# An attention, scan and expert pipeline on one core: query, key and value projections placed elsewhere, and the stages up to the first scan put in another order

## The chip, the cores and the metric

The kernel runs on one core of a Trainium2 chip. The metric is the device time of one execution, in microseconds (us); lower is better. Before the change three runs took 1169.0, 1170.27 and 1170.85 us, median 1170.27 us.

## What is computed

Two layers over four batches of 512 tokens with 256 features, all in float32. The part that matters here is the head of layer 0:

```
qkv = x @ w_qkv.T + b_qkv                    # 4 batches, 16 heads of 16
attn = softmax(q @ k.T / 4)                  # 512 x 512 for each head
h = (attn @ v) @ w_out.T + b_out
h = concatenate([h, txt])                    # 512 + 77 tokens
u = layernorm(h); xp = u @ x_proj_w.T
delta = softplus(xp[..., :64] @ dt_proj_w.T + dt_proj_b)
state = exp(delta * A) * state + delta * B * u       # scan over 589 tokens, 16 states
h = h + sum(state * C) + u * D_skip
```

Behind it come an expert layer of 14 experts (layer 0), a causal attention and an expert layer of 128 experts with two experts per token (layer 1). The change doesn't touch them.

## The kernel before

Every engine has its own program, written out by hand; semaphores join them. Nothing is reordered by a scheduler: on each engine an instruction that waits holds up everything behind it.

For each batch `b` the heads are worked in four groups `hg` of four heads, and a group in four units of 128 queries (16 units a batch, `NU`). A unit has two **sets** `g` of two heads; a set fills two of PSUM's eight banks. The steps are:

- **Projections** (TensorE, `project`, L657): Q (`which` 0) and K (`which` 1) of a group, two matmuls each (four passes in the trace); ScalarE evicts them with their bias (`take_q`, L1251). V comes in two halves (`project_v`, L667; `take_v`, L1255). x of a batch lies in the one tile `xT`, and SP loads the next batch's over it once all projections of the batch are made (`load_x`).
- **Scores and maxima**: `scores` (L686) makes a set, VectorE takes its negated row maxima (`maxima`, L1682). With three bank sets (`SETS`) TensorE may be three sets ahead; for most of batch 1 there are only two sets. After a group, `turn_maxima` (L701) transposes the maxima and `minus` (L1687, VectorE) adds them to Q's spare rows.
- **Turned scores and weighted sums**: `tscores` (L766) makes the scores again, transposed and with the maximum taken off, `exps` (L1305, ScalarE) takes the exponential, `weighted` (L779) multiplies with V into bank 4, and `take_o` (L1309) evicts it after a group. `turn_heads` (L796), `values`, `turn_values`, `project_out` and `residual` (L1762, VectorE) finish the attention.
- **Chain to the scan**: `moments`, `standard_deviations`, `normalise`, `turn_tokens` (L711), `take_u`, `project_x` (L718), `take_x`, `project_dt` (L725), `softplus` (L1281 to L1288, ScalarE), `step_size` (L1710), `input_size`.
- **Scan** (VectorE): for each of 16 states `drive` (L1724), `recurrence` (L1733) and `output_gate` (L1743); `decay` (L1296, ScalarE) makes its factors, SP broadcasts its rows.

The stages, with their functions: `first_front` (scores and maxima of batch 0 with its projections), `first_back` (turned scores of batch 0, with batch 1's projections and first scores), `first_chain` (the rest of batch 0's chain between the scores of batch 1, units 4 to 15), `back_ahead(1, 0)` (the scan of batch 0 on VectorE, while TensorE and ScalarE do the turned scores of batch 1), then `front(2, 1)`, `back_ahead(2, 1)`, `front(3, 2)`, `back_ahead(3, 2)`, the last scan, and the later layers. In `front(mb, nb)` VectorE takes all the maxima of batch `mb`, while TensorE also turns y of batch `nb - 1` at units 7, 9 and 11 (`turn_both`, L843). `back_ahead` projects Q and K of the next batch's groups 0 to 2 near its end, into banks 5 to 7; group 3 and V are projected in the front.

In the first front both projections of the next group stand whole behind units 1 and 2:

```
if i in (1, 2):
    if hg + 1 < HG:
        project(b, hg + 1, i - 1)
    else:
        project_v(b, i - 1)
```

## Time and profile before

| | |
|---|---|
| median of three runs | 1170.27 us |
| the profiled execution | 1173.3 us, span 1171.5 us |
| TensorE matmul busy | 918.4 us, 78% of the span |
| TensorE weight load busy | 505.3 us, 43% |
| VectorE busy | 762.7 us, 65% |
| ScalarE busy | 443.0 us, 38% |
| GpSimd busy | 204.6 us, 17% |
| mean granted TensorE clock | 0.849 of full |

The shares are averages over stages with different limits. The span is the time from the first to the last instruction of the profiled execution; its own time, 1173.3 us, is 1.8 us more. In the rows below, PE is TensorE's matmul, PEld its weight load, DVE VectorE, ACT ScalarE, SP the engine that issues most DMAs. A float32 matmul has two passes and so two entries.

### The profile page before, as it was taken

What the parts mean: (1) busy time and instruction counts of PE and PEld (TensorE: products, weight loads), DVE (VectorE), ACT (ScalarE), POOL (GpSimd) and SP (SyncE); (2) the same over time, 40 slices, a digit from 0 to 9 for tenths busy, and PEclk for the clock granted to TensorE, in tenths of its full rate; (3) what the DMA queues carried; (4) which work ended last, traced back from release to release, by engine and by line L of the source; (5) the groups of instructions that cost most, each with busy time, mean ns of one, the idle gap of its engine ahead of it and who ended that gap; (6) DMA issues with size and microseconds to landing.
All of it is one profiled execution on the core that took longest, in us unless ns stands there. A gap on an engine that the chain in (4) does not pass through costs nothing. (4 is left out here: it accounts for less than half of the span.)

```text
span 1171.5 us, 14347 instructions
## 1 busy us (share of the span) xinstructions
PE 918.4 (78%) x4632; PEld 505.3 (43%) x4633; DVE 762.7 (65%) x1351; ACT 443.0 (38%) x822; POOL 204.6 (17%) x248
## 2 busy tenths in 40 slices
PE   7899889978988888975576539999489898529980
PEld 2323432242522434223353239999266666414440
DVE  4802569999799997999899931111366767833325
ACT  1156226952169521783452214444123313302220
POOL 1000000111001100011000142333000023246660
PEclk9989877986879869796686859999699988759995
DMA  3099123987039760487666446665600500229957
GB/s 104 11 334 319 59 83 101 216 197 169 1 110 236 182 155 1 119 217 182 178 205 210 146 154 190 196 199 161 242 1 1 218 22 15 75 81 376 400 206 264
DMA packets 75403, 185.57 MB, mean 158 GB/s; under 512 B 12154, under 2 KB 48717, under 8 KB 72656
## 3 DMA queue, kind: packets, MB, share of 16 engines
q1 hardware_dynamic: 60944, 148.11, 37.9%
q0 software_dynamic: 14400, 36.71, 14.4%
q8 instruction: 33, 0.54, 0.2%
q14 instruction: 26, 0.21, 0.1%
HBM read 124.88 MB, written 43.69 MB: 144 GB/s over the span
## 5 line engine op out<-in xcount | busy, mean ns | idle before, releaser
L1682 DVE TENSOR_REDUCE mxn<-ps 128x2 f32<-128x1024 f32 x128 | 150.3, 1219 | 92.2 <-PE ps L686 92.0
L1733 DVE TENSOR_TENSOR_SCAN hst<-dA,dBu 128x1180 f32<-128x1180 f32 x64 | 166.9, 2608 | 0.5
L1305 ACT ACTIVATE Ph<-ps 128x1024 f32<-128x1024 f32 x128 | 125.5, 1075 | 37.1 <-PE ps L766 36.6
L686 PE MATMUL ps<-Kh,Qh 32*128 32x512 f32 x512 | 118.8, 750 | 16.7 <-DVE mxn L1682 13.2
L766 PE MATMUL ps<-Qh,Kh 32*128 32x512 f32 x512 | 118.6, 732 | 1.9 <-ACT Ph L1305 1.8
L1724 DVE TENSOR_TENSOR dBu<-dtu,bc 128x1180 f32<-128x1180 f32 x64 | 88.1, 1381 | 6.7 <-DMA bc<-bc_dram 6.3
L1619 POOL DMA_DIRECT2D yS<-hC x24 | 20.8, 866 | 409.4 <-DVE hC L1743 409.4
L1743 DVE TENSOR_TENSOR hC<-hst,bc 128x1180 f32<-128x1180 f32 x64 | 86.8, 1362 | 0.0
L2043 DVE TENSOR_TENSOR yo<-ps,b2r 128x256 f32<-128x256 f32 x32 | 13.6, 424 | 105.9 <-PE ps L1020 105.9
L1296 ACT ACTIVATE dA<-delta,acol 128x590 f32<-128x590 f32 x64 | 52.2, 816 | 71.3 <-DVE hst L1733 63.2
L779 PE MATMUL ps<-Ph,Vh 128*32 128x512 f32 x512 | 74.1, 653 | 5.2 <-ACT OT L1309 3.3
L1221 PE MATMUL ps<-ring,xgT 128*64 128x256 f32 x512 | 71.0, 400 | 0.1
L2300 DVE COPY yo<-ps 128x256 f32<-128x256 f32 x64 | 27.2, 424 | 66.6 <-PE ps L1221 66.6
L657 PE MATMUL ps<-xT,wqk 128*128 128x512 f32 x128 | 63.7, 637 | 7.4 <-DMA wqk<-in_wqk 5.2
L1671 POOL DMA_INDIRECT ys_dram<-yo,dest x64 | 62.3, 973 | 40.2 <-issue 23.5
L1651 POOL DMA_INDIRECT xs_dram<-xa,to x40 | 39.6, 989 | 167.4 <-DVE to L2142 154.8
L766 PEld LDWEIGHTS ps<-Qh,Kh 32*128 32x128 f32 x512 | 35.5, 207 | 77.0 <-ACT Ph L1305 41.7
L686 PEld LDWEIGHTS ps<-Kh,Qh 32*128 32x128 f32 x512 | 35.3, 214 | 76.2 <-DVE mxn L1682 49.3
L1010 PEld LDWEIGHTS ps<-xgT,W 128*128 128x128 f32 x512 | 63.4, 195 | 3.2 <-ACT xgT L1450 1.6
L1010 PE MATMUL ps<-xgT,W 128*128 128x128 f32 x512 | 63.9, 279 | 1.0 <-ACT xgT L1450 1.0
L788 PE MATMUL ps<-hC,ident 128*128 128x512 f32 (+1 forms) x96 | 47.7, 647 | 18.2 <-DVE hC L1743 18.2
L1020 PE MATMUL ps<-W,hidT 128*128 x256 | 60.5, 380 | 0.0
(266 smaller groups left out, 1428.8 us busy)
## 6 DMA issues: line engine op xcount, KB each, us to landing
bc<-bc_dram SPq DMA_DIRECT2D x64, 590.0 KB, 5.1
ring<-in_we SPq DMA_DIRECT2D x16, 2048.0 KB, 14.0
W<-in_w SPq DMA_DIRECT2D x46, 512.0 KB, 4.0
yS<-hC POOLq DMA_DIRECT2D x24, 590.0 KB, 6.9
yodd<-hC POOLq DMA_DIRECT2D x24, 590.0 KB, 7.1
xs_dram<-zeros SPq DMA_DIRECT2D x1, 8224.0 KB, 42.7
xg<-xs_dram SPq DMA_DIRECT2D x16, 514.0 KB, 10.9
ys_dram<-zeros SPq DMA_DIRECT2D x1, 5120.0 KB, 47.6
```

The lines of the kernel that those rows point to most:

```text
L657: m = nc.tensor.matmul(ps[:, bank, :], wqk[:, hg, which, c, :], xT[:, c, :], start=(c == 0), stop=(c == KC - 1))
L686: m = nc.tensor.matmul(ps[:, banks.start + hh % 2, :], Qh[HR * hh:HR * (hh + 1), hg, P * i:P * (i + 1)], Kh[HR * hh:HR * (hh + 1), hg, :], ...
L766: m = nc.tensor.matmul(ps[:, banks.start + hh % 2, :], Kh[HR * hh:HR * (hh + 1), hg, P * j:P * (j + 1)], Qh[HR * hh:HR * (hh + 1), hg, :], ...
L779: m = nc.tensor.matmul(ps[HR * hh:HR * (hh + 1), 4, :], Vh[:, j, 4 * hg + hh, :], Ph[:, n % 2, hh, :], start=(j == 0), stop=(j == QT - 1))
L1010: m = nc.tensor.matmul(ps[:, 2 + u, P * f:P * (f + 1)], W1[:, v, c, P * f:P * (f + 1)], xgT[:, u, c, :], start=(c == 0), stop=(c == KC - 1))
L1221: t = nc.tensor.matmul(ps[CAP * k:CAP * (k + 1), 2 + j % 4, 0:D], xgT5[:, j % 2, c, CAP * k:CAP * (k + 1)], weights_of(g % PLACES)[:, 2 * ...
L1305: nc.scalar.activation(Ph[:, n % 2, 2 * g:2 * g + 2, :], ps[:, turned_banks(b, 2 * n + g), :], ACT.Exp, scale=float(HD) ** -0.5).then_inc( ...
L1671: nc.gpsimd.indirect_dma_start(ys5_dram, bass.IndirectOffsetOnAxis(dest5[:, j:j + 1], 0), yo5[:, j // GP % YG, j % GP, :], None, bounds_ch ...
L1682: nc.vector.tensor_reduce(slots32(mxn[:, hg % 2, i, :])[:, 2 * g:2 * g + 2, HD], ps[:, score_banks(b, 2 * u + g), :], AX.X, ALU.max, negat ...
L1724: nc.vector.tensor_tensor(dBu[:, k % 2, :, :], dtu[:, :, :], bc[:, k % SLOTS, 0:1, :].to_broadcast([P, KC, LP]), ALU.mult).then_inc(dve_dB ...
L1733: nc.vector.tensor_tensor_scan(hst[:, k % 2, :, :].rearrange("p c t -> p (c t)"), dA[:, k % 2, :, :].rearrange("p c t -> p (c t)"), dBu[:, ...
L1743: nc.vector.tensor_tensor(gated(k), hst[:, k % 2, :, :], bc[:, k % SLOTS, 1:2, :].to_broadcast([P, KC, LP]), ALU.mult).then_inc(dve_hC, 1)
```

## The change

Seven things, all in the order of the programs and in the PSUM banks:

1. `project` and `project_v` are cut into parts of one matmul (`project_part`) and one tile pair (`project_v_part`); in the first front one part stands behind each unit. Batch 0's maxima are turned in bank 7, its projections stay in bank 4.
2. Batch 0's turned scores wait for the last maxima of their own banks, not for all; units 0 to 7 use three bank sets. The turn of group 3's maxima stands behind unit 0's turned scores.
3. `turn_heads` of group 3 comes behind a set of batch 1's scores.
4. In the first chain Q3 and K3 of batch 1 stand inside units 5 and 6, `project_dt` is cut in two around a set of scores, V's halves stand behind units 9 and 10 (before: 13 and 14), and VectorE's `step_size` and `input_size` behind units 12 and 13 (before: 10 and 11).
5. For batches 2 and 3, Q3 is projected behind Q and K of groups 0 to 2, K3 behind `turn_tokens`, and V's first half behind `project_dt`, all in `back_ahead` of the batch ahead.
6. V's second half stands behind unit 0 in `front`.
7. ScalarE's evictions follow: `take_v(mb, 0)` behind `softplus`, `take_v(mb, 1)` first in the front.

The core of the diff:

```
+        def q_bank(b, hg, which):
+            if b == 0:
+                return 4 if hg else which
+            if b == 1:
+                return 7
+            return gap_bank(hg, which) if hg < QG else (4, 3)[which]
+
+        def v_bank(b):
             return 7 if b == 1 else 4
+
+        def turn_bank(b):
+            return 7 if b < 2 else 4
...
+        def turned_set(b, v):
+            return SETS[v % 2] if b == 0 and v >= NU else SETS[v % 3]
...
+            def project_part(b, hg, which, c):
+                bank = q_bank(b, hg, which)
+                if c == 0:
+                    if hg == 0 and which == 0:
...
+                    elif b >= 2:
+                        if which == 0:
+                            pe.wait_ge(act_ot, HG * b)
+                        else:
+                            pe.wait_ge(dve_vals, 2 * b)
...
+            def project_v_part(b, half, i):
+                if i == 0:
+                    if half:
+                        pe.wait_ge(act_v, 2 * b + 1)
+                    elif b == 0:
+                        pe.wait_ge(act_q, 2 * HG)
+                    elif b >= 2:
+                        pe.wait_ge(act_q, 2 * (HG * b + QG) + 1)
...
+                elif b >= 2 and v == 1:
+                    pe.wait_ge(act_q, 2 * HG * (b + 1))
...
+                if b < 2 and hg:
+                    pe.wait_ge(dve_q, HG * b + hg)
+                if b == 1:
+                    if hg > 1:
+                        pe.wait_ge(act_v, 2 * b + 2)
+                    else:
+                        pe.wait_ge(act_q, 2 * (HG * b + QG + hg))
+                elif b >= 2:
                     pe.wait_ge(act_v, 2 * b + 2)
...
+                    if hg + 1 < HG:
+                        project_part(b, hg + 1, i // 2, i % 2)
+                    else:
+                        project_v_part(b, i // 2, i % 2)
...
-                if n == 0:
+                if n == 0 and b:
...
-                    if v >= turned_sets(b):
-                        pe.wait_ge(act_p, 2 * NU * b + v + 1 - turned_sets(b))
+                    if turned_free(b, v):
+                        pe.wait_ge(act_p, turned_free(b, v))
+                    elif b == 0:
+                        pe.wait_ge(dve_max, last_maxima(b, v))
...
+                    else:
+                        turn_maxima(0, HG - 1)
...
-                turn_heads(0, range(HG))
+                turn_heads(0, range(QG))
+                scores(1, 4, 0)
+                turn_heads(0, range(QG, HG))
 
             def first_chain():
-                scores(1, 4, 0)
-                turn_maxima(1, 0)
                 turn_values(0, 0)
                 turn_values(0, 1)
                 scores(1, 4, 1)
+                turn_maxima(1, 0)
                 project_out(0, 0)
                 project_out(0, 1)
-                unit_scores(1, 5)
-                unit_scores(1, 6)
+                scores(1, 5, 0)
+                project(1, 3, 0)
+                scores(1, 5, 1)
+                scores(1, 6, 0)
+                project(1, 3, 1)
+                scores(1, 6, 1)
                 turn_tokens(0, low)
                 unit_scores(1, 7)
                 project_x(0, low)
+                scores(1, 8, 0)
                 turn_maxima(1, 1)
-                unit_scores(1, 8)
-                unit_scores(1, 9)
-                project_dt(0, low)
-                project(1, 3, 0)
+                scores(1, 8, 1)
+                project_dt_part(0, low, 0)
+                scores(1, 9, 0)
+                project_dt_part(0, low, 1)
+                scores(1, 9, 1)
+                project_v(1, 0)
                 unit_scores(1, 10)
-                project(1, 3, 1)
-                unit_scores(1, 11)
-                for u in range(12, NU):
+                project_v(1, 1)
+                for u in range(11, NU):
                     unit_scores(1, u)
                     if u == 12:
                         turn_maxima(1, 2)
-                    elif u in (13, 14):
-                        project_v(1, u - 13)
                 turn_maxima(1, 3)
...
-                    if i in (1, 2):
-                        if hg + 1 == QG:
-                            project(mb, QG, i - 1)
-                        elif hg + 1 == HG:
-                            project_v(mb, i - 1)
+                    if u == 0:
+                        project_v(mb, 1)
...
+                    project(eb + 1, QG, 0)
                 room = low if eb == NB - 1 else tail
                 turn_tokens(eb, room)
+                if eb < NB - 1:
+                    project(eb + 1, QG, 1)
                 project_x(eb, room)
                 project_dt(eb, room)
+                if eb < NB - 1:
+                    project_v(eb + 1, 0)
...
             def first_chain():
                 take_vals(0, 0)
                 take_vals(0, 1)
+                take_q(1, 3, 0)
                 standard_deviations(0)
                 normalise(0)
+                take_q(1, 3, 1)
                 take_u(0, low)
                 take_x(0, low)
                 softplus(0, low)
-                take_q(1, 3, 0)
-                take_q(1, 3, 1)
-                begin_sum(0)
                 take_v(1, 0)
                 take_v(1, 1)
+                begin_sum(0)
                 decay(0, 0)
 
             def front(mb, nb):
+                take_v(mb, 1)
                 decay(nb, 0)
-                take_q(mb, 3, 0)
-                take_q(mb, 3, 1)
-                take_v(mb, 0)
                 begin_sum(nb)
-                take_v(mb, 1)
 
...
+                            take_q(eb + 1, QG, 0)
                     if n == 13:
                         take_u(eb, room)
+                        if eb < NB - 1:
+                            take_q(eb + 1, QG, 1)
                     if n == 14:
                         take_x(eb, room)
                 softplus(eb, room)
-                if eb == NB - 1:
+                if eb < NB - 1:
+                    take_v(eb + 1, 0)
+                else:
...
-                maxima(1, 4, 0)
+                unit_maxima(1, 4)
                 minus(1, 0)
-                maxima(1, 4, 1)
                 residual(0)
                 moments(0)
                 maxima(1, 5, 0)
...
                     unit_maxima(1, u)
                     if u % QT == 0:
                         minus(1, u // QT - 1)
-                    if u == 10:
+                    if u == 12:
                         step_size(0)
-                    elif u == 11:
+                    elif u == 13:
                         input_size(0)
```

How the rows of TensorE's program move, at three places. In the first front (from the turn of group 0's maxima to that of group 1's, with group 2's projections; L657 and L682 are Q and K projections, L686 and L729 scores, L701 and L749 the turn of maxima), before:

```order
L701 MATMUL ps<-ident,mxn 128x128 x4
L686 MATMUL ps<-Kh,Qh 128x512 x4
L657 MATMUL ps<-xT,wqk 128x512 x2
L686 MATMUL ps<-Kh,Qh 128x512 x4
L657 MATMUL ps<-xT,wqk 128x512 x2
L686 MATMUL ps<-Kh,Qh 128x512 x8
L701 MATMUL ps<-ident,mxn 128x128 x4
```

and now:

```order
L749 MATMUL ps<-ident,mxn 128x128 x4
L682 MATMUL ps<-xT,wqk 128x512
L729 MATMUL ps<-Kh,Qh 128x512 x4
L682 MATMUL ps<-xT,wqk 128x512
L729 MATMUL ps<-Kh,Qh 128x512 x4
L682 MATMUL ps<-xT,wqk 128x512
L729 MATMUL ps<-Kh,Qh 128x512 x4
L682 MATMUL ps<-xT,wqk 128x512
L729 MATMUL ps<-Kh,Qh 128x512 x4
L749 MATMUL ps<-ident,mxn 128x128 x4
```

Each of the two projections has become two parts, one behind each of the group's four units.

In the first chain (L711 and L759 turn the tokens, L718 and L766 project x, L725 and L772 project dt), before:

```order
L711 MATMUL ps<-ident,xn 128x128 x10
L686 MATMUL ps<-Kh,Qh 128x512 x4
L718 MATMUL ps<-uT,xpw 96x512 x2
L718 MATMUL ps<-uT,xpw 96x78 x2
L701 MATMUL ps<-ident,mxn 128x128 x4
L686 MATMUL ps<-Kh,Qh 128x512 x8
L725 MATMUL ps<-xpo,dtw 128x512
L725 MATMUL ps<-xpo,dtw 128x78
L725 MATMUL ps<-xpo,dtw 128x434
L725 MATMUL ps<-xpo,dtw 128x156
L657 MATMUL ps<-xT,wqk 128x512 x2
L686 MATMUL ps<-Kh,Qh 128x512 x4
```

and now:

```order
L682 MATMUL ps<-xT,wqk 128x512 x2
L729 MATMUL ps<-Kh,Qh 128x512 x4
L682 MATMUL ps<-xT,wqk 128x512 x2
L729 MATMUL ps<-Kh,Qh 128x512 x2
L759 MATMUL ps<-ident,xn 128x128 x10
L729 MATMUL ps<-Kh,Qh 128x512 x4
L766 MATMUL ps<-uT,xpw 96x512 x2
L766 MATMUL ps<-uT,xpw 96x78 x2
L729 MATMUL ps<-Kh,Qh 128x512 x2
L749 MATMUL ps<-ident,mxn 128x128 x4
L729 MATMUL ps<-Kh,Qh 128x512 x2
L772 MATMUL ps<-xpo,dtw 128x512
```

The projections of Q3 and K3 have moved from behind dt to before the turn of the tokens, and a set of scores stands wherever two blocks stood together; the second half of dt and V follow.

At the end of the first scan and the start of front 2 (L667 and L701 with wv are V), before:

```order
L657 MATMUL ps<-xT,wqk 128x512 x12
L711 MATMUL ps<-ident,xn 128x128 x10
L718 MATMUL ps<-uT,xpw 96x512 x2
L718 MATMUL ps<-uT,xpw 96x78 x2
L725 MATMUL ps<-xpo,dtw 128x512
L725 MATMUL ps<-xpo,dtw 128x78
L725 MATMUL ps<-xpo,dtw 128x434
L725 MATMUL ps<-xpo,dtw 128x156
L686 MATMUL ps<-Kh,Qh 128x512 x20
L701 MATMUL ps<-ident,mxn 128x128 x4
L686 MATMUL ps<-Kh,Qh 128x512 x12
```

and now:

```order
L682 MATMUL ps<-xT,wqk 128x512 x14
L759 MATMUL ps<-ident,xn 128x128 x10
L682 MATMUL ps<-xT,wqk 128x512 x2
L766 MATMUL ps<-uT,xpw 96x512 x2
L766 MATMUL ps<-uT,xpw 96x78 x2
L772 MATMUL ps<-xpo,dtw 128x512
L772 MATMUL ps<-xpo,dtw 128x78
L772 MATMUL ps<-xpo,dtw 128x434
L772 MATMUL ps<-xpo,dtw 128x156
L701 MATMUL ps<-wv,xT 128x256 x4
L729 MATMUL ps<-Kh,Qh 128x512 x4
L701 MATMUL ps<-wv,xT 128x256 x4
```

Two matmuls more (Q3) stand in the run of projections, K3 behind the turned tokens, V's halves around unit 0's scores.

## Rows read from the trace of the kernel before

**Rows 1.** Busy time by stage: stretch, its length, each engine's busy time, clock, DMA.
```profile
core 0: us, PE busy (x) PEld busy (x) DVE busy (x) ACT busy (x) POOL busy (x), PEclk, DMA share, GB/s
13.60:59.70 46.10, 39.98 (x182) 15.35 (x181) 39.25 (x36) 5.32 (x8) 0.00 (x0) 1.00 0.05 14
...
89.00:121.40 32.40, 32.40 (x184) 10.23 (x180) 9.46 (x8) 19.44 (x23) 0.00 (x0) 1.00 1.08 324
...
121.40:183.30 61.90, 52.40 (x210) 24.91 (x210) 38.93 (x52) 18.04 (x28) 0.00 (x0) 0.80 0.15 52
...
183.30:273.30 90.00, 76.78 (x358) 27.97 (x350) 87.28 (x69) 65.47 (x87) 12.59 (x15) 0.86 0.74 176
...
268.40:286.00 17.60, 13.58 (x42) 4.16 (x41) 17.60 (x14) 6.52 (x8) 2.58 (x3) 0.59 0.88 204
```

**Rows 2.** Waits of VectorE, 14-60, 123-183, 273-329 us: total, times, longest.
```profile
DVE mxn L1682 <- PE ps L686: 6.5, 9, 0.9
...
DVE mxn L1682 <- PE ps L686: 18.6, 9, 7.9
...
DVE mxn L1682 <- PE ps L686: 8.1, 4, 3.9
```

**Rows 3.** Timeline, first front: start, duration, engine, line, what, [idle before <- releaser].
```profile
25.63 0.66 PE L701 MATMUL ps<-ident,mxn 128*128 128x128 f32 x4
...
30.39 1.14 PE L686 MATMUL ps<-Kh,Qh 32*128 32x512 f32 x8
...
31.47 1.98 PE L657 MATMUL ps<-xT,wqk 128*128 128x512 f32 x4
...
33.38 1.99 PE L686 MATMUL ps<-Kh,Qh 32*128 32x512 f32 x12
...
34.23 0.31 PEld L686 LDWEIGHTS ps<-Kh,Qh 32*128 32x128 f32 x4 [0.54 <-ACT Kh L1251]
...
34.55 4.62 DVE L1682 TENSOR_REDUCE mxn<-ps 128x2 f32<-128x1024 f32 x4 [0.63 <-PE ps L686]
...
39.09 0.68 DVE L1687 TENSOR_TENSOR Qh<-Qh,ps 128x512 f32<-128x512 f32 x1
```

**Rows 4.** Timeline, from the first front to the first back stage.
```profile
59.66 0.59 PE L701 MATMUL ps<-ident,mxn 128*128 128x128 f32 x3 [2.45 <-DVE mxn L1682]
...
62.58 1.94 ACT L1305 ACTIVATE Ph<-ps 128x1024 f32<-128x1024 f32 x2 [5.80 <-PE ps L766]
```

**Rows 5.** Timeline, units 3 to 8 of the first back stage.
```profile
75.93 1.07 PE L779 MATMUL ps<-Ph,Vh 128*32 128x512 f32 x8
...
76.93 1.98 PE L657 MATMUL ps<-xT,wqk 128*128 128x512 f32 x4
...
88.44 1.95 PE L766 MATMUL ps<-Qh,Kh 32*128 32x512 f32 x8 [0.27 <-ACT Ph L1305]
```

**Rows 6.** Timeline, first chain, up to the first scan.
```profile
123.30 1.13 PE L686 MATMUL ps<-Kh,Qh 32*128 32x512 f32 x4
...
150.97 4.46 PE L725 MATMUL ps<-xpo,dtw 64*128 64x512 f32 x8
...
155.37 3.78 PE L657 MATMUL ps<-xT,wqk 128*128 128x512 f32 x4
...
159.41 1.19 ACT L1288 ACTIVATE sp<-sp 128x1180 f32<-128x1180 f32 x1
...
160.25 2.36 DVE L1682 TENSOR_REDUCE mxn<-ps 128x2 f32<-128x1024 f32 x2 [7.93 <-PE ps L686]
...
162.52 1.38 DVE L1710 SCALAR_TENSOR_TENSOR delta<-xb,sp 128x1180 f32<-128x1180 f32 x1
...
183.29 2.68 DVE L1724 TENSOR_TENSOR dBu<-dtu,bc 128x1180 f32<-128x1180 f32 x2
```

**Rows 7.** Timeline, end of the first scan and front of batch 2.
```profile
272.46 1.19 ACT L1288 ACTIVATE sp<-sp 128x1180 f32<-128x1180 f32 x1
...
305.28 1.88 PE L657 MATMUL ps<-xT,wqk 128*128 128x512 f32 x4
...
308.26 2.35 DVE L1682 TENSOR_REDUCE mxn<-ps 128x2 f32<-128x1024 f32 x2 [2.66 <-PE ps L686]
```

More of the change, by code:

```diff
@@ new lines, in project @@
+            def project(b, hg, which):
+                for c in range(KC):
+                    project_part(b, hg, which, c)
+            def project_v_part(b, half, i):
[7 more added lines that the diff above has]
+                    else:
+                        pe.wait_ge(dve_q, HG * b + (HG - 2 if b == 1 else HG - 1))
+                for c in range(KC):
+                    m = nc.tensor.matmul(ps[:, v_bank(b), D * i:D * (i + 1)], xT[:, c, P * (2 * half + i):P * (2 * half + i + 1)], wv[:, c, :],
+                                         start=(c == 0), stop=(c == KC - 1))
+                if i == 1:
+                    m.then_inc(pe_v, 1)
@@ L669, in project_v @@
-                m.then_inc(pe_v, 1)
+                    project_v_part(b, half, i)
             def scores(b, u, g):
@@ L677, in scores @@
                     pe.wait_ge(dve_max, freed_by(b, v))
+                elif b == 1 and v == 0:
+                    pe.wait_ge(act_p, NU - 1)
                 elif b == 1 and v == 2 * QT + 1:
@@ L1245, in take_q @@
             def take_q(b, hg, which):
-                if b >= 2 and hg < QG:
-                    bank = gap_bank(hg, which)
-                else:
-                    bank = which if b == 0 and hg == 0 else misc_bank(b)
+                bank = q_bank(b, hg, which)
                 act.wait_ge(pe_q, 2 * (HG * b + hg) + which + 1)
```

91 lines of the change are left out of this document (42 added, 49 removed).

## Prediction

> **What bounds the kernel now.** I read the table of busy time by stage first. From 13.6 to 59.7 us VectorE, which takes the row maxima of batch 0's scores, works 39.3 of 46.1 us; in the first chain (121.4 to 183.3 us) 38.9 of 61.9; in the first scan (183.3 to 273.3 us) 87.3 of 90.0 [rows 1]. So a scan is bound by VectorE itself, while the stages ahead of the first scan have time in which it only waits. The page's chain of waits does not help: it names only the last stages. The later stages follow from the first scan without slack, so what the first 183 us lose or win should reach the end whole.
>
> The view of waits says for whom VectorE waits: for TensorE's scores, 6.5 us in the first front, 18.6 in the first chain, 8.1 in each later front [rows 2]. The reader should see in the timeline how: VectorE needs about 1.15 us for a set (4.62 for four), TensorE 1.08 for a unit of two sets and then 1.91 for a whole projection in between (from 31.47 to 33.38), and after it VectorE has stood still, for 0.63 us before the four maxima at 34.55 [rows 3]. In between, from 88.44 to 121.4 us, TensorE is busy all the time: 32.4 of 32.4 us [rows 1, 5].
>
> **First front.** Each projection of batch 0 is now made in two parts, one after each unit. Full and half clock (1.98 and 3.78 us for four passes) say that 1.80 of the time goes with the clock and some 0.15 is fixed [rows 3, 6], so a part costs 1.05, between 0.96 (half of 1.91) and 1.08. TensorE's period for a group of four units: 4 x 1.08 + 4 x 1.05 + 0.66 for turning the maxima + 0.85 of waiting until ScalarE has evicted K (the row at 34.23 against the next issue at 33.38) = 10.0 [rows 3]. VectorE's: 8 x 1.14 (from 34.55 to 39.09 for four) + 0.6 to 0.7 = 9.7 [rows 3]. So TensorE is still 0.3 too slow in the first three groups. Of the nine waits, 6.5 us in all [rows 2], the one before the very first maxima stays (a ninth, 0.7), and of the 5.8 left some 0.6 do, two of the three times 0.3: **-5.2**, bounds -4.0 and -5.8.
>
> **Switch and first half of the back stage.** Before, the last maximum ends at 59.6, its turn is made, the first exponential starts at 62.58 [rows 4], and the scores of unit 8 start at 88.44 [rows 5]: 28.8 us. Now the first turned scores wait for the last maxima only of their own banks, the turn comes after them, and three bank sets serve units 0 to 7 in place of two. From the last maximum: 1.15 for the second set, 0.66 for the turn, 7 x (1.07 + 1.00) for scores and weighted products (starts of 75.93 and 76.93 differ by 1.00), 2 x 1.91 for the projections of batch 1 [rows 3, 5] = 20.1. I add 1.9: 1.0 for unit 8, whose first set now waits for the exponential of unit 7's second set, and 0.9 for ScalarE's evictions. That is 22.0: **-6.8**, bounds -4 (the old pace returns after the start) and -8.7 (nothing added). Units 8 to 15 keep their two sets and TensorE their bound: 0.
>
> **First chain.** Its worst wait is 7.93 us at 160.25: TensorE has made the whole dt projection (4.46 at half clock) and a projection of Q (3.78) with no scores ready for VectorE [rows 6]. Now Q3 and K3 stand before the chain's token turn, dt comes in two halves, and V's halves stand at units 10 and 11. I walked the order from W, the end of the last weighted product, at full clock, with 1.91 for a projection, 1.08 for a pair of sets and as much for a set alone (the row at 123.30 has one set in 1.13, the one at 30.39 two in 1.14) [rows 3, 6], and half of the half-clock duration for other blocks. Heads are turned at W+3.0, about 1.1 later than before, since a set of scores is put between; outputs at 10.6; units 5 and 6, split around Q3 and K3, end at 19.1; tokens 20.6; x 24.0; dt 30.2. Then the first V half may be read only after ScalarE's softplus, about 5.2 us (from the end of dt at 155.43 to 160.60) [rows 6]: V's second half starts at 36.0, unit 11's scores end at 39.0. Behind them ten maxima (11.4), two subtractions, two operations of 1.4 on the step size and the last turn: the first drive of the scan at W+55.4 against 61.9 before (121.4 to 183.3) [rows 1, 6]. That is -6.5 at full clock. The old stage had a granted clock of 0.80 [rows 1]; the new one fills the gap behind the residual with Q3, so it should be better off, yet I leave 1.5: **-5.0**, bounds -1 (half clock in the long blocks again) and -8.
>
> **Ends of scans, fronts 2 and 3.** Q3, K3 and V0 go to the end of the preceding scan, behind the projections that are made there. They cost nothing there: TensorE waits for ScalarE around the token turn, and the scan is VectorE's; ScalarE's three evictions, under 0.85 us each, fit, since each decay is made a whole step of the scan (90.0 / 16 = 5.6 us) ahead [rows 1, 3]. SP's queue gains: the load of the next x no longer waits until the middle of the front. In the front the 1.88 us projection ahead of the wait of 2.66 us at 308.26 goes; what is late next there is the turn of y, so I keep 0.8 of it; of the two small waits (8.1 - 3.9 - 2.66 = 1.5) I take 0.6 [rows 2, 7]: -2.5. Against it stands a new wait: V's second half is the second thing in the front, and it needs V's first half evicted, which ScalarE does only behind the softplus that ends at 273.65 (272.46 + 1.19), so at 274.3 [rows 7]. Behind it on TensorE stand unit 1's scores, for which VectorE comes at 277.0 (two maxima and the step size after 273.3). At full clock V takes 1.9 and the scores 1.1: 277.4, a loss of 0.5. At half clock V takes 3.7 and the scores 1.1 to 1.7: 279.5, a loss of 2.6. I take half clock, since the clock granted from 268.4 to 286.0 is 0.59 although TensorE was busy 13.6 of these 17.6 us [rows 1]: +2.5. Per front **0**, bounds -2.5 and +1.5.
>
> The Trainium skill says otherwise: on its page "TensorE: Matmul & The Clock Gate", section "What's actually happening", the throttled clock is the default and activity releases it. By that V, which comes soon after an unbroken run of projections, would find 2.4 GHz, and both fronts together would give 4 us more; the trace of this place, 0.59 (the level of 1.2 GHz most of the time) right after such a run, speaks for the low level.
>
> **Sum.** -5.2 - 6.8 - 5.0 + 0 = -17.0. The profiled execution took 1173.3 us (span 1171.5), 3.0 above the median of the three runs; I carry the difference over to the median: 1170.3 - 17.0 = **1153.3**.
>
> **Rivals.**
> - *The chain gives little.* TensorE falls to half clock in the new chain too, at the wait for softplus or in the split units; each projection of 1.91 then costs 1.9 more. For it speaks the old stage's 0.80 [rows 1], against it the shorter waits. The chain gives 1 and the switch 5: 1170.3 - 11.2 = 1159.
> - *The fronts win.* V's second half meets the full clock: 1153.3 - 4 = 1149.3. This is also the time by the skill's rule.
> - *The shift does not arrive.* A transfer with a time of its own (the zero fill, the broadcasts) sets the scan's start: 1170. Against it: the DMA share in the old chain is 0.15, so the fill is long over [rows 1].
> - *Slower.* In the first front TensorE now goes between 32-row score matmuls and full ones twice as often. If that drops the granted clock there from 1.00 to 0.5, a group costs 4 x 1.7 + 4 x 1.95 + 1.3 + 0.85 = 16.8 in place of some 11.2 now (9.7 and a quarter of the waits), so +22 over four groups instead of -5.2: 1170.3 + 22 - 11.8 = 1180. With 5.6 lost in each slow group and 1.3 won in each other, it decides from the third slow group of the four. Against it: the old front, with as many kinds of matmul and less work, had 1.00 all along [rows 1].
>
> **How the numbers follow.** Forecast 0.56 (1149.5 to 1157), the chain gives little 0.20, the fronts win 0.16, no arrival 0.04, slower 0.04. The bounds of the terms added fully would reach from 1142 to 1165; as they will not all fall on one side, I cut to 1146 to 1162, which leaves out no change, slower, and a tenth beside. A change of 0.2%, 2.3 us, is about what a measurement of this kernel can tell from none. Faster 0.92, same 0.04, slower 0.04.
>
> **What would show it.** Right: the turn of batch 0's last maxima near 54.3 us, waits of VectorE below 1.5 us in that front; unit 8's turned scores near 76; the first drive of the scan near 166, with no wait of VectorE above 3 us in the chain; in fronts 2 and 3 the wait of 2.66 gone, and a wait of 0.5 to 3 us before unit 1's maxima. The scans keep their 90 and 88 us. Wrong: a granted clock under 0.9 in the first front, scores of units 0 to 7 still 3 us apart, or a scan that grows by what the stages before it won.

## The result, and the profile after

The changed kernel took 1155.52 us (median of four runs, 1148.68 to 1157.98) and the kernel before 1170.56 us on the same chip (four runs, 1169.0 to 1176.12): a ratio of 0.9869, 95% interval 0.9828 to 0.9911. That is 15.3 us faster, between 10.5 and 20.1. The forecast was 1153.3 us.

The profiled execution of the changed kernel is its fastest run, 1148.68 us (span 1146.8, mean granted clock 0.868), and that of before was above its median, so the two traces differ by 24.7 us. I use the traces for where the time went, and the ratios for how much. The table of busy time by stage, which answers to [rows 1]: first front, the two halves of the back stage, first chain, scan, front 2, scan, front 3.

```profile
core 0: us, PE busy (x) PEld busy (x) DVE busy (x) ACT busy (x) POOL busy (x), PEclk, DMA share, GB/s
15.20:56.00 40.80, 38.25 (x176) 14.21 (x176) 38.50 (x35) 5.32 (x8) 0.00 (x0) 1.00 0.01 1
56.00:83.10 27.10, 25.05 (x154) 7.43 (x156) 0.82 (x3) 19.40 (x22) 0.00 (x0) 1.00 1.07 331
83.10:112.20 29.10, 29.10 (x165) 9.06 (x161) 9.48 (x8) 17.09 (x20) 0.00 (x0) 1.00 1.10 299
112.20:167.50 55.30, 48.02 (x210) 22.82 (x210) 38.88 (x51) 18.14 (x28) 0.00 (x0) 0.92 0.33 116
167.50:258.60 91.10, 79.72 (x372) 30.43 (x365) 87.52 (x69) 67.34 (x90) 12.61 (x15) 0.88 0.74 174
258.60:311.70 53.10, 43.84 (x188) 20.09 (x190) 45.83 (x55) 5.29 (x9) 1.09 (x2) 0.74 0.28 79
311.70:400.80 89.10, 78.59 (x374) 30.02 (x367) 87.37 (x71) 67.45 (x90) 12.39 (x15) 0.90 0.74 178
400.80:452.50 51.70, 42.63 (x185) 18.07 (x187) 45.76 (x55) 5.29 (x9) 1.05 (x2) 0.80 0.26 71
```

VectorE's work in the first chain is the 38.9 us that it was; the stage is 55.3 us long instead of 61.9, at a granted clock of 0.92 instead of 0.80. The scans kept their 90 us. Set side by side, with the stages bounded by the first and last maxima, the first turn of heads and the first drive, and the third scan by batch 3's step size (the predicted differences are the terms of the sum):

| stage | before | after | difference | predicted |
|---|---|---|---|---|
| first front | 44.81 | 40.85 | -3.96 | -5.2 |
| back stage | 61.79 | 56.15 | -5.64 | -6.8 |
| first chain | 61.89 | 55.36 | -6.53 | -5.0 |
| fronts 2 and 3 | 55.31, 55.32 | 53.02, 51.69 | -2.3, -3.6 | 0, 0 |
| three scans | 90.05, 88.03, 91.9 | 91.09, 89.14, 89.77 | 0.0 in all | 0 |
| from there to the end | 607.6 | 604.5 | -3.1 | 0 |

The last row is work that the change does not touch; I leave it out below. (The first maxima start 0.4 us later in the second trace, which makes up the rest of the 24.7.) The view of waits of VectorE, which answers to [rows 2], for the first front, the first chain, front 2 and front 3:

```profile
DVE mxn L1743 <- PE ps L729: 2.8, 4, 0.8
...
DVE mxn L1743 <- PE ps L729: 10.7, 9, 2.3
...
DVE mxn L1743 <- PE ps L729: 5.9, 3, 3.9
...
DVE mxn L1743 <- PE ps L729: 4.6, 4, 1.5
```

The waits for scores fell from 6.5 to 2.8, from 18.6 to 10.7 and from 8.1 to 5.9 and 4.6 us. Three of the four that are left in the first front look like this in the timeline (start, duration, engine, line, what, and in brackets the idle time before and what ended it):

```profile
32.64 1.12 PE L682 MATMUL ps<-xT,wqk 128*128 128x512 f32 x2
33.80 0.69 ACT L1310 ACTIVATE Kh<-ps,bqk 128x512 f32<-128x512 f32 x1 [4.36 <-PE ps L682]
34.54 1.14 PE L729 MATMUL ps<-Kh,Qh 32*128 32x512 f32 x8 [0.78 <-ACT Kh L1310]
...
35.72 2.36 DVE L1743 TENSOR_REDUCE mxn<-ps 128x2 f32<-128x1024 f32 x2 [0.75 <-PE ps L729]
```

K's last part stands at the end of a group, the scores of the next group need it evicted, and VectorE pays 0.75 us for that once a group.

Of the twelve runs that follow, the first eight were made on two other chips, on which every kernel takes some 25 us more, the one before too (medians 1196.78 and 1194.38 us). Nearly all of that lies behind the third scan, spread over the later layers, the causal attention included. The last four ran on a chip with the times of the first one (before: 1169.36 us). So across kernels I compare ratios to before, and durations of the head stages, which agree between the chips to 0.05 us where the clock does.

### The profile page after: what moved, and what is told of

It is laid out like the page before. It is cut to its first block, busy times and chain, and to the rows that moved or that the text cites. A ratio compares the mean times of both kernels' runs of the same rounds, so it can differ in the third digit from the quotient of the medians.

```text
span 1146.8 us, 14354 instructions
## 1 busy us (share of the span) xinstructions
PE 904.8 (79%) x4632; PEld 497.5 (43%) x4633; DVE 762.6 (66%) x1351; ACT 442.3 (39%) x822; POOL 204.8 (18%) x248
## 4 chain that ended last, share of the span: by engine, by line
DVE 34%; PE 30%; issue 19%; DMA 10%; POOL 4%; ACT 1%; SPq 1%; POOLq 0%; DVEq 0%
DVE hst L1794 11%; DVE mxn L1743 5%; PE ps L729 5%; PE ps L1283 4%; DMA bc<-bc_dram 4%; PE ps L1159 3%; DVE hC L1804 3%; PE ps L682 2%; POOL ys_dram L1701 2%; PE ps L1231 2%; DVE dBu L1785 2%; DMA xg<-xs_dram 2%; PE ps L818 2%; DMA yodd<-hC 2%; PE ps L1271 2%
## 5 line engine op out<-in xcount | busy, mean ns | idle before, releaser
L729 PE MATMUL ps<-Kh,Qh 32*128 32x512 f32 x512 | 120.6, 726 | 12.2 <-DVE mxn L1743 9.8
L818 PE MATMUL ps<-Qh,Kh 32*128 32x512 f32 x512 | 116.0, 725 | 2.4 <-ACT Ph L1364 2.1
L682 PE MATMUL ps<-xT,wqk 128*128 128x512 f32 x128 | 63.8, 632 | 5.6 <-DMA wqk<-in_wqk 5.6
L729 PEld LDWEIGHTS ps<-Kh,Qh 32*128 32x128 f32 x512 | 36.3, 207 | 72.0 <-DVE mxn L1743 44.4
```

The lines of the kernel that those rows point to most:

```text
L682: m = nc.tensor.matmul(ps[:, bank, :], wqk[:, hg, which, c, :], xT[:, c, :], start=(c == 0), stop=(c == KC - 1))
L729: m = nc.tensor.matmul(ps[:, banks.start + hh % 2, :], Qh[HR * hh:HR * (hh + 1), hg, P * i:P * (i + 1)], Kh[HR * hh:HR * (hh + 1), hg, :], ...
L818: m = nc.tensor.matmul(ps[:, banks.start + hh % 2, :], Kh[HR * hh:HR * (hh + 1), hg, P * j:P * (j + 1)], Qh[HR * hh:HR * (hh + 1), hg, :], ...
```

## The experiments

Theory: the sum of the prediction, stage by stage. Rivals: the gain comes from one stage alone, or from TensorE's clock and not from the order of the work.

**The changed kernel again**, to see which stages repeat. No edit.

> The changed kernel itself, to see how much its own time and stages move from one execution to the next. Theory (the gain is made of stages that are all bound by the same few waits): its median stays near 1155 us, and the first scan starts at 167 to 168 us in this trace too. Rival (the profiled execution of 1148.7 us was a lucky one, with a transfer or the clock in a better phase in the later stages): the start of the first scan is the same, but the stretch from there to the end is 3 to 8 us longer than the 979 us of that execution.

Measured: 1177.38 us, ratio 0.9866 (0.9822 to 0.9909). Front and back stage are 40.85 and 56.15 us again, to the hundredth. The chain is not: 58.58 us in place of 55.36. TensorE's busy time and granted clock in this run, at its start,

```profile
core 0: us, PE busy (x), PEclk, DMA share, GB/s
112.00:117.00 5.00, 3.79 (x25) 0.97 1.09 386
117.00:122.00 5.00, 5.00 (x15) 0.50 1.09 385
122.00:127.00 5.00, 5.00 (x19) 0.84 0.36 128
```

stand against these of the first profile of the same program,

```profile
112.00:117.00 5.00, 3.79 (x28) 1.00 1.09 387
117.00:122.00 5.00, 5.00 (x28) 1.00 0.84 298
122.00:127.00 5.00, 4.94 (x17) 1.00 0.03 9
```

and the timeline of this run shows the place, where TensorE waits 1.21 us for VectorE's values and then goes on at half clock:

```profile
116.19 1.71 PE L858 MATMUL ps<-ident,vals 128*128 128x128 f32 x8 [1.21 <-DVE vals L1816]
...
117.82 2.08 PE L729 MATMUL ps<-Kh,Qh 32*128 32x512 f32 x4
...
120.74 5.01 PE L865 MATMUL ps<-wo,valsT 128*128 128x256 f32 x16
```

In the first profile the same rows are 1.25, 1.13 and 3.62 us, behind the same wait of 1.21. So the wait is always there and the clock falls behind it only at times.

The rival of this run, that the first profiled execution was a lucky one, is borne out by later profiles. From the first drive to the end that execution took 979.3 us. Two runs below, with the early exponential and with two sets on top of it, have the same program from there on and ran on a chip as fast; they took 986.9 and 984.6 us, and the kernel before 988.2. This run's own 1004.3 us can't be used for it, since the 25 us of its chip are in it.

**Only batches 2 and 3**: the kernel before with parts 5 to 7 of the change alone.

```
+                    if u == 0:
+                        project_v(mb, 1)
...
+                    project(eb + 1, QG, 0)
                 turn_tokens(eb, room)
+                if eb < NB - 1:
+                    project(eb + 1, QG, 1)
                 project_x(eb, room)
                 project_dt(eb, room)
+                if eb < NB - 1:
+                    project_v(eb + 1, 0)
```

> The kernel before with only the moves for batches 2 and 3 (Q3, K3 and V's first half at the end of the preceding scan, V's second half behind unit 0). My sum had 0 here (-2.5 for the projections gone, +2.5 for V's second half at half clock): 1170 us. The rival, V's second half at full clock: each front 2.5 to 3.5 us shorter, no wait of VectorE before unit 1's maxima, 1164 to 1166 us. If the scans grow by what the fronts win, 1170 with fronts of 52 us.

Measured: 1191.81 us, ratio 0.9979 (0.9951 to 1.0007), which time alone cannot tell from no change. In the trace the fronts are 53.06 and 52.47 us, where every profile with the old fronts shows 54.9 to 55.7. VectorE has no wait before unit 1's maxima in either, which is the rival's picture, though V's second half ran at half clock (3.47 us) in the first of them.

**Only the stages up to the first scan**: the changed kernel with batches 2 and 3 as before (the same lines taken back).

> The changed kernel with batches 2 and 3 as before: only the new stages up to the first scan. The first scan starts at 167 to 168 us; fronts 2 and 3 take 55.3 us again. By the sum of the trace after (15.7 us won by then) 1155 to 1157 us; if part of that is given back in the first scan, whose broadcasts now meet other transfers, 1157 to 1160.

Measured: 1186.23 us, ratio 0.991 (0.9876 to 0.9944). Fronts 2 and 3 are 55.67 and 54.88 us again. The head stages are the changed kernel's: 40.85, 56.14, and a chain of 58.47 with the clock at 0.74 from 112 to 122 us.

**Only the split projections**: the kernel before with part 1 of the change alone; no early switch, no third set, the old chain.

```
+                    if hg + 1 < HG:
+                        project_part(b, hg + 1, i // 2, i % 2)
+                    else:
+                        project_v_part(b, i // 2, i % 2)
```

> The kernel before with only the first front changed: each projection of batch 0 in two parts, one behind each unit, its maxima turned in another bank. I forecast -5.2; the trace after shows the last maximum of batch 0 at 56.0 us against 59.6, so -3.6 to -4.0: 1166 to 1167 us. If the back stage with two bank sets follows at its old pace, the first scan starts about 4 us earlier; if it waits for something else there, less.

Measured: 1188.71 us, ratio 0.9946 (0.9915 to 0.9977). The front is 40.85 us, as in the full change. But the back stage, whose order is untouched, went from 61.79 to 57.99. The granted clock says why: before it is

```profile
60.00:72.00 12.00, 10.64 (x45) 0.57 1.10 321
```

and in this run

```profile
60.00:72.00 12.00, 12.00 (x68) 1.00 1.10 285
```

Before, TensorE stands idle for 2.45 us ahead of the last turn of maxima [rows 4]; here the wait is 1.25, and no fall follows it.

**The clock alone**: the kernel before with ten passes of work that nothing reads, put into that idle time.

```
+                for _ in range(5):
+                    nc.tensor.matmul(ps[:, 7, :], ident[:, :], Kh[:, 0, :], start=True, stop=True)
                 turn_maxima(b, HG - 1)
```

> The kernel before with five matmuls of 128x512 more (ten passes, some 2.3 us at full clock, their result is read by nothing) right before the last turn of batch 0's maxima, where TensorE stands idle for 2.45 us. No work is taken away. Theory A (what the split gained in the back stage is TensorE's clock, which fell after that idle time): the granted clock stays at 1.00 from 60 to 72 us, the back stage takes 58.0 to 59.5 us in place of 61.79, the first maxima and their end stay where they are (59.6), and the time falls by 2.3 to 3.8 us (ratio 0.997 to 0.998). Theory B (the gain came from the order of the work, not from the clock): the back stage stays at 61.5 to 62.2 us and the time is that of the kernel before, or up to 0.5 us longer.

Measured: 1197.67 us, ratio 1.0006 (0.9976 to 1.0036). The extra passes took 4.56 us, not 2.3 (I had mis-sized them), and pushed the turn back by 1.9:

```profile
57.34 4.56 PE L753 MATMUL ps<-Kh,ident 128*128 128x512 f32 x10
...
61.74 0.60 PE L701 MATMUL ps<-ident,mxn 128*128 128x128 f32 x4
```

```profile
60.00:72.00 12.00, 10.83 (x61) 1.00 1.10 295
```

Yet the back stage is 59.80 us, 2.0 shorter than before, with more work in it and 1.9 us of delay at its head. So the full clock is worth 3.9 us there, which is what the split showed (3.80). So theory A holds for the stage. For the time it is not shown: the expected ratio was 0.997 to 0.998, and the measured interval contains that and no change too.

**Two bank sets in place of three** for units 0 to 7, the rest as changed.

```
-            return SETS[v % 2] if b == 0 and v >= NU else SETS[v % 3]
+            return SETS[v % 2] if b == 0 else SETS[v % 3]
```

> The changed kernel, but units 0 to 7 of batch 0's turned scores use two bank sets (as before) in place of three; everything else as changed. It tells the early switch and the split apart from the third set. Between the last maximum of batch 0 and the end of its last weighted product lie 61.79 us before, 56.15 after, and 57.99 with the split projections alone. Theory A (the split gives 3.8 because TensorE keeps its full clock, and the third set gives most of the rest): the back stage goes back to 57.3 to 58.0 us, the scan of batch 0 starts 1.2 to 1.8 us later, the time is 1 to 2 us above the changed kernel's (ratio to before 0.988). Theory B (the early switch of the first turned scores gives the rest, the third set is worth nothing): the back stage stays within 56.1 to 56.6 us, the time is the same.

Measured: 1184.78 us, ratio 0.9885 (0.984 to 0.9929). The back stage took 61.55 us: neither theory. TensorE waited 1.93 us for the first exponential, and its clock fell behind that:

```profile
59.54 2.99 PE L818 MATMUL ps<-Qh,Kh 32*128 32x512 f32 x8 [1.93 <-ACT Ph L1364]
```

```profile
60.00:72.00 12.00, 12.00 (x60) 0.72 1.10 283
```

So this run did not tell what the third set is worth; it raised the question of why the first exponential comes so late.

**The turn of maxima inside the wait for the values**, in the first chain.

```
+                turn_maxima(1, 0)
                 turn_values(0, 0)
                 turn_values(0, 1)
                 scores(1, 4, 1)
-                turn_maxima(1, 0)
```

> The changed kernel, but in the first chain the turn of batch 1's first maxima (0.66 us) stands ahead of the turns of the values, that is in the wait of 1.2 us for VectorE's values, instead of two places behind. Theory A (the chain took 58.5 us in two of three profiles because TensorE's clock falls for a while after that wait, and 55.4 where it did not): TensorE waits only 0.5 to 0.7 us there, its granted clock is 1.00 from 112 to 124 us and the chain takes 55.0 to 55.6 us every time; time 1 to 3 us below the changed kernel's mean (ratio to before 0.984 to 0.986). Theory B (the clock falls whatever the length of that wait): the chain takes 58 us again in some profiles; the time falls by no more than the 0.6 us by which project_out comes earlier.

Measured: 1180.55 us, ratio 0.9867 (0.9821 to 0.9913). The chain took 54.96 us. The wait is 0.77:

```profile
118.03 1.25 PE L858 MATMUL ps<-ident,vals 128*128 128x128 f32 x8 [0.77 <-DVE vals L1816]
```

Over all profiles of this study, the order with the wait of 1.21 us had the half clock behind it in three of six (chains of 58.47 to 58.58 us; the others 55.36 to 55.38), the order with 0.77 in none of four (54.96, 56.61, 54.97 and 54.96 us; the 56.61 has its half clock later, at 149 to 152 us). With so few, the second may be luck, and the ratio shows no gain over the changed kernel: in this same run the clock fell at another place, behind a wait of 0.87 us at the head of the back stage (57.75 us in place of 56.15).

**The turn of y in parts**: the run before, and in fronts 2 and 3 five parts of 128 tokens in place of three blocks.

```
+        TURNS = (6, 10, 12)
+        Y_PARTS = {5: (0, 0), 6: (0, 1), 9: (1, 0), 10: (1, 1), 12: (2, 0)}
...
-                    if u in TURNS:
-                        turn_both(nb - 1, TURNS.index(u))
+                    if u in Y_PARTS:
+                        turn_both_part(nb - 1, *Y_PARTS[u])
```

> The kernel of the run before, and in fronts 2 and 3 the turn of y is cut by 128 tokens: five parts behind units 5, 6, 9, 10 and 12 in place of three blocks behind units 7, 9 and 11; VectorE adds them behind units 7, 11 and 13. The first block stood in the way of unit 8's scores: VectorE waited 3.89 us there, with TensorE at half clock. Theory A (the fronts are now bound by single long blocks of TensorE only): that wait shrinks to under 1.6 us, and fronts 2 and 3 take 49.5 to 50.8 us in place of 51.7 to 53.0; time 4 to 5 us below the kernel of the run before (ratio 0.980 to 0.982). Theory B (the clock, not the block, sets the wait, and the parts find half clock at two places in place of one): the waits of VectorE add up to the same 3.5 to 4 us in each front and the time stays within 1 us.

Measured: 1172.77 us, ratio 0.9786 (0.9742 to 0.9829). The fronts are 48.57 and 48.50 us, 3.5 less than in the run before (51.67 and 52.29), better than expected (49.5 to 50.8). The mean granted clock in front 2 is 0.83 in the run before and 0.82 in this one, so the clock does not explain it. The parts also stand behind other units than the blocks did, and this run does not tell the cut and the new places apart. In the changed kernel VectorE stood still ahead of unit 8, while TensorE turned y:

```profile
279.96 0.80 PE L896 MATMUL ps<-ident,yS 128*128 128x128 f32 x2
...
285.19 2.36 DVE L1743 TENSOR_REDUCE mxn<-ps 128x2 f32<-128x1024 f32 x2 [3.89 <-PE ps L729]
```

Now the waits of VectorE for scores in front 2 are, in all,

```profile
DVE mxn L1749 <- PE ps L730: 1.6, 2, 1.2
```

**The early exponential.** The row of ScalarE in the changed kernel had the answer to the question above:

```profile
55.06 2.17 PE L818 MATMUL ps<-Qh,Kh 32*128 32x512 f32 x8 [0.22 <-DVE mxn L1743]
...
58.46 0.17 DVE L2376 TENSOR_SCALAR acol<-acol 128x32 f32<-128x32 f32 x1
58.67 3.77 ACT L1364 ACTIVATE Ph<-ps 128x1024 f32<-128x1024 f32 x4 [3.19 <-DVE acol L2376]
```

ScalarE waits, ahead of its back stage, for a change of sign that VectorE makes behind the last subtraction of the first front. Before the change that wait cost nothing, since the turned scores came later still. The edit moves it to the first use:

```
-            act.wait_ge(dve_init, 1)
             first_back()
...
                 begin_sum(0)
+                act.wait_ge(dve_init, 1)
                 decay(0, 0)
```

> The changed kernel with one wait of ScalarE moved. In the profile of the changed kernel the first exponential starts at 58.67 us, although its scores are there from some 56.2 on: ScalarE waits for VectorE's change of sign of acol (58.46 + 0.17), which stands on VectorE behind the last subtraction of the first front and is needed only in the scan. The wait now stands before the first decay. Theory A (that wait kept the early switch from arriving, and it makes the idle time of 0.87 us on TensorE, after which its clock fell in one of the profiles): the first exponential starts 0.2 to 0.5 us after the last maximum of batch 0 instead of 2.63, TensorE has no idle time there, and the stage from the last maximum to the turn of the heads takes 54.6 to 55.3 us in place of 56.15; time 1 to 1.5 us below the changed kernel's (ratio to before 0.985 to 0.986). Theory B (TensorE's own work binds the stage from its start, the exponentials only fill in): 56.0 to 56.2 us, no gain.

Measured: 1153.51 us against 1169.36, ratio 0.9845 (0.9816 to 0.9874). The first exponential starts 0.18 us after the last maximum, TensorE's idle time of 0.87 us is gone, and the back stage is 54.32 us, 1.83 shorter. The ratio's interval overlaps that of the changed kernel, so the gain is shown in the stage and not in the time; this profile also has the half clock in its chain (58.46 us):

```profile
55.51 2.08 ACT L1364 ACTIVATE Ph<-ps 128x1024 f32<-128x1024 f32 x2 [0.75 <-PE ps L818]
56.44 0.66 PE L749 MATMUL ps<-ident,mxn 128*128 128x128 f32 x4
57.03 1.14 PE L818 MATMUL ps<-Qh,Kh 32*128 32x512 f32 x8
```

The same with **two sets**, now at full clock:

> The same with two bank sets in place of three for units 0 to 7. In the earlier run with two sets TensorE's clock fell at the switch, so it did not tell what the third set is worth. Here the exponentials start early, so that fall should not come. Theory A (the third set is worth 1.5 to 2 us at full clock, since with two sets TensorE waits for an exponential in each unit): stage of 56.3 to 57.2 us, 1.5 to 2 us longer than the run beside it. Theory B (what the third set gave was the early scores of unit 1 alone): within 0.5 us of the run beside it. If the clock falls all the same, TensorE shows 0.50 in a stretch behind 58 us and the stage is over 58 us.

Measured: 1156.82 us, ratio 0.9882 (0.9851 to 0.9913). The back stage is 56.68 us, so the third set is worth 2.36 us in the stage, more than the 1.5 to 2 of theory A:

```profile
59.23 1.63 PE L818 MATMUL ps<-Qh,Kh 32*128 32x512 f32 x8
...
61.79 1.79 PE L818 MATMUL ps<-Qh,Kh 32*128 32x512 f32 x8
```

A pair of sets that takes 1.14 us without a wait takes 1.63 and 1.79 here, because it waits for an exponential in its middle.

**All three edits together** (the turn of maxima, y in parts, the early exponential):

> The kernel with the turn of y in five parts and the turn of maxima in the wait for the values, with the same wait of ScalarE moved. Both gains should add, since one lies ahead of the first scan and the other behind it: stage behind the last maximum 54.6 to 55.3 us, fronts 2 and 3 at 48.6 us as in that kernel; ratio to before 0.977 to 0.978. If the stages ahead of the scan no longer reach the end (a transfer sets the start of the scan), the ratio stays at 0.979 and the first scan starts no earlier or grows by the gain.

Measured: 1144.77 us against 1169.36, ratio 0.9773 (0.9744 to 0.9803). Front, back stage and chain are 40.84, 54.33 and 54.97 us, the fronts 48.8 and 49.2. This version is faster than both kernels: by that ratio 26.5 us less than before (between 23 and 30), where the changed kernel has 15.3.

**K between the sets**: the run before, with K's last part between the two sets of unit 3.

```
+                    scores(b, u, 0)
+                    if i == QT - 1 and hg + 1 < HG:
+                        project_part(b, hg + 1, 1, 1)
+                    scores(b, u, 1)
```

> The run before, with the last part of each K projection of the first front set between the two sets of its unit instead of behind them. In the changed kernel TensorE waits 0.78 us for K's eviction at the head of each new group, and VectorE then 0.75 us for its scores, three times. Theory A (that eviction is the last thing late there): TensorE's wait falls to 0.2 to 0.3, VectorE's to 0.1 to 0.3, and the first front takes 39.2 to 39.7 us in place of 40.85. Theory B (the period of TensorE's own work, 10.0 us by my sum against VectorE's 9.7, is what is late): 40.6 to 40.9 us, the wait only changes its place. Time in the first case 1.1 to 1.6 us below the run before (ratio 0.976 to 0.977).

Measured: 1144.77 us, ratio 0.9786 (0.9753 to 0.9819), no gain. The first front is 41.22 us, 0.4 longer, outside both ranges. VectorE's wait is 0.89 us instead of 0.75, now one set earlier:

```profile
34.42 1.99 PE L730 MATMUL ps<-Kh,Qh 32*128 32x512 f32 x12
34.53 0.69 ACT L1320 ACTIVATE Kh<-ps,bqk 128x512 f32<-128x512 f32 x1 [3.95 <-PE ps L683]
35.27 0.31 PEld L730 LDWEIGHTS ps<-Kh,Qh 32*128 32x128 f32 x8 [0.55 <-ACT Kh L1320]
35.60 3.49 DVE L1753 TENSOR_REDUCE mxn<-ps 128x2 f32<-128x1024 f32 x3 [0.89 <-PE ps L730]
```

The set that K's part pushed back is the late one. This run decides between the theories less well than it was meant to. The weights of the next group's scores still wait for K's eviction (the row at 35.27), so that wait did not go. And the edit added work: a set that stands alone takes 1.13 us, as in [rows 6], where two sets together take 1.14, so that each pair taken apart costs TensorE up to 1 us more. What it shows is that K's part can't be had earlier for nothing.

## Why the prediction was right, and where it was not

The sum was -17.0 and the measured difference -15.3, so the forecast held. Its terms were less good than their sum.

**First front, -5.2.** It gave -3.96, and 40.84 to 40.86 us in every profile with that order. The step that was too small is the wait left in each group: I took "two of the three times 0.3"; it is 0.80, 0.75 and 0.75. The period of a group is 10.53 us (maxima start at 25.18, 35.72 and 46.25), where the text had 10.0. That sum laid TensorE's blocks end to end and let it wait for K's eviction alone. In the trace TensorE, up to three sets ahead, also waits inside the group until VectorE has freed a bank: the unit at 39.19 takes 1.72 us up to K's part at 40.91 where one without that wait takes 1.07.

```profile
39.19 1.80 PE L729 MATMUL ps<-Kh,Qh 32*128 32x512 f32 x8
...
39.85 0.30 PEld L729 LDWEIGHTS ps<-Kh,Qh 32*128 32x128 f32 x4 [0.37 <-DVE mxn L1743]
```

So neither engine's own work is the period; they wait for each other in turn, through the banks and through K. No run takes one of these waits away alone.

**Switch and first half of the back stage, -6.8.** Unit 8's turned scores start 23.7 us after the last maximum (79.74 against 56.04), where the text had 22.0, and 28.8 before: -5.1 there, and -0.5 in the rest. The size was near, the make-up was wrong. Of the 5.64 us, 3.8 come with the split alone, through the clock: TensorE's idle time ahead of the last turn shrinks from 2.45 to 1.25 us, and it does not fall to half clock for the following 10 us. I had the row with the 2.45 us [rows 4] and never asked what the clock did behind it. Against that, the failing step is "the first turned scores wait only for the last maxima of their own banks": they do, but their exponential started 2.62 us after the last maximum, and 0.18 in the run without the wait for acol, so it came 2.4 us late for a constant made on another engine. The 1.0 us that the text allowed for unit 8 was right: it waits 1.18 us for an exponential. With that wait out of the way the stage is 54.32 us, that is -7.5. Three sets against two are 2.36 of them (56.68 against 54.32).

**First chain, -5.0.** The walk at full clock gave W+55.4, and the profile 55.36; the 1.5 us of allowance was for a fall of the clock, and that fall is there in half of the profiles and costs 3.1 to 3.2 us. Six profiles of this order average 56.9 us, four of the old one 60.8 (59.60 to 61.89): -3.9 on the mean. I took 61.9 as the old length from one profile, which was the longest of the four. V's second half starts 35.8 us behind the start of the stage, after 1.64 us of waiting for the first one's eviction, where the walk had 36.0, and no wait of VectorE in the chain is above 2.9 us.

**Ends of scans and fronts, 0.** Here the term was wrong, in the direction of the rival "the fronts win": 14 fronts of the changed order average 52.83 us, the eight of the old order 55.25, so -2.4 each. The wait of 2.66 is gone, as the text says. The new wait never came. The failing step is the one that put softplus's end 0.3 us behind the scan's; in the changed kernel it ends ahead of it, and V starts before the first maxima:

```profile
256.48 1.19 ACT L1347 ACTIVATE sp<-sp 128x1180 f32<-128x1180 f32 x1
257.57 0.58 ACT L1314 ACTIVATE Vh<-ps 128x512 f32<-128x512 f32 x1
258.20 1.99 PE L701 MATMUL ps<-wv,xT 128*128 128x256 f32 x8 [2.70 <-ACT Vh L1314]
258.64 2.35 DVE L1743 TENSOR_REDUCE mxn<-ps 128x2 f32<-128x1024 f32 x2
```

I had read that distance from the kernel before, where TensorE came to x's projection out of an idle stretch at half clock (3.94 us); with K3 ahead of it it takes 2.28. The change moved the time that I used as fixed. V's second half ran at 1.99 us in nine of twelve fronts of full-change orders and at 3.08 to 3.52 in three. The price of 2.6 us for half clock was wrong too: in the front with 3.08 VectorE goes on without a wait and the whole front is 51.69 us; in one with 3.30 it lasts 54.95 us, but VectorE's first wait (1.15 us) comes at 274.08, 13 us after V, and the longest (4.11) at the turn of y. The scores behind V are made ahead of their need. (The two longest of the twelve fronts, 55.01 and 54.95 us, are two of the three with V at half clock. Their extra time lies at the turn of y and behind it, and whether V's clock has a part in it is not shown.)

The rule cited from the Trainium skill's page "TensorE: Matmul & The Clock Gate", section "What's actually happening" (activity releases the throttle), foresaw this side, and the traces agree in nine of the twelve. In three of those nine it is V's first half that ran at half clock (3.55 to 3.68 us). What I set against the rule was misread: the granted clock of 0.59 is that of 268.4 to 286.0 us, while the run of projections had ended at 256.2 us, and TensorE had stood idle for 2.73 and 1.24 us right behind it and for 1.70 and 1.61 us inside that stretch. So it was no evidence about work right behind an unbroken run. Nor do these fronts test that cleanly: V's second half comes behind an idle time, of 2.70 us in nine of the twelve (the clock fell in three of these) and of 1.01 to 1.08 in the three with V's first half at half clock.

**The rivals.** "The shift does not arrive" and "slower" are out: from the first drive to the last output gate the three scans take 269.0 us together on the mean of seven profiles with the changed fronts and 269.2 on that of four with the old ones, and the granted clock in the first front is 1.00 with the split. "The chain gives little" is half true: the fall of the clock it describes happens at times, at another place than it named, and costs 3 us, not 4.

**The sum again**, with the means over the profiles of each order: -4.0 - 5.3 - 3.9 - 4.8 = -18.0 (the back stage is 56.15 us in four of five profiles and 57.75 in the one in which the clock fell). That is inside the interval of the measured -15.3 (-20.1 to -10.5); where the 2.7 us between them went is open. The two errors, fronts too pessimistic by 4.8 and the rest too hopeful by 3.8 on these means, stood against each other, so that the total came out so near is in part luck.

## What to carry to other kernels

When a stage is to start earlier, walk every engine's list up to its first instruction there, waits for constants included: a wait that was covered for free (acol) becomes the one that decides, and here it held back 1.8 us and made an idle time of 0.87 us for TensorE. When one long block stands between short ones that another engine needs, cut it and spread it: that gave 4.0 us in the first front and, with new places for the parts, 3.5 in each later one. And read what the clock did behind each idle time of the busiest engine before you price the work that follows; a duration or a distance taken from the old trace holds only where the change leaves the clock ahead of it alone.

## What the runs showed of the hardware

- The granted clock can fall after short waits of TensorE, and not each time. Behind idle times of 2.45 us (kernel before, and again in the run with batches 2 and 3 alone) and 1.93 us (two sets) it showed 0.50 for the next 10 and 7 us; behind 1.21 us in three of six profiles; behind 0.87 us in one of five; behind 1.25 us, ahead of the last turn in the run with the split alone, it stayed at 1.00. Behind 2.70 us, ahead of V's second half, it fell in three of nine fronts. The same program, with starts that agree to 0.4 us up to there, gave chains of 55.36 and 58.58 us.
- Filling an idle time with useless matmuls can shorten what follows: 4.56 us of them, 1.9 us of which delayed the stage, still left it 2.0 us shorter.
- Two sets of 32-row score matmuls that stand next to each other took 1.14 us together, and one set alone 1.13 us, so the second is nearly free only while nothing stands between them.
